# A row of a state-space scan's slot moves from VectorE to GpSimd

## The reference

```python
xn = _layernorm(x)
x_norm = _layernorm(xn, ln_in_g, ln_in_b)
x_norm = x_norm + conv(x_norm)
gate, input_gate = split(x_norm @ gate_w.T + gate_b)
Bm = x_norm * sigmoid(input_gate) @ B_w.T + B_b
Cm = x_norm @ C_w.T + C_b
A_bar = expm(dt_A * A)
def step(state, bc):                 # state: (8, 64)
    b_t, c_t = bc
    s = _layernorm(state @ A_bar + b_t, ln_st_g, ln_st_b)
    return (s, c_t * s)
ssm = scan(step, 0, (Bm, Cm))        # 2048 steps
s = (ssm @ D_w.T + D_b) * sigmoid(gate)
out = x + s * silu(xn @ W.T + b + (xn @ V_r) @ C.T)
```

## Time and profile before

| | us |
|---|---|
| median of 2 executions | 2489.38 (2488.64 to 2490.12) |
| profiled execution | 2491.04 |
| its span | 2489.2 |
| TensorE busy (matmul) | 2448.6 (98%) |
| VectorE busy | 2189.7 (88%) |
| ScalarE busy | 1013.5 (41%) |
| GpSimd busy | 1242.5 (50%) |
| DMA, share of 16 engines | 20% |

### The profile page before, as it was taken

One profiled execution on the slowest core, in us unless ns is written; L12 is line 12 of the kernel. 1 busy time (PEld: TensorE's weight loads), 2 busy tenths in 40 slices (PEclk: granted clock), 3 DMA queues, 4 the chain that ended last, 5 costly groups with the idle time before them and its releaser, 6 DMA issues.

```text
span 2489.2 us, 42423 instructions
## 1 busy us (share of the span) xinstructions
PE 2448.6 (98%) x10031; PEld 1307.4 (53%) x10031; DVE 2189.7 (88%) x10934; ACT 1013.5 (41%) x1859; POOL 1242.5 (50%) x2433
## 2 busy tenths in 40 slices
PE   8999999999999999999999999999999999999996
PEld 4555555555555555555555555555555555555544
DVE  6788889988889988889988899888899888899887
ACT  5444333444433444434443434443344444334310
POOL 2444555545555545555545555445555455555443
PEclk9999999999999999999999999999999999999998
DMA  3112211212212122112122112122112122121121
GB/s 113 24 47 56 60 41 41 52 47 60 57 33 52 48 52 60 45 39 58 49 52 60 43 41 55 48 56 60 38 44 52 47 60 53 36 53 48 35 59 36
DMA packets 99678, 125.14 MB, mean 50 GB/s; under 512 B 31975, under 2 KB 48743, under 8 KB 99432
## 3 DMA queue, kind: packets, MB, share of 16 engines
q1 hardware_dynamic: 98560, 121.12, 20.2%
q10 hardware_dynamic: 872, 1.31, 0.2%
HBM read 71.96 MB, written 33.55 MB: 42 GB/s over the span
## 4 chain that ended last, share of the span: by engine, by line
POOL 33%; PE 33%; DVE 24%; issue 9%; ACT 1%; DMA 0%; POOLq 0%; SPq 0%; DVEq 0%; ACTq 0%
POOL dw L429 30%; DVE wq L942 10%; PE bank L1256 7%; DVE dw L969 7%; DVE dw L955 7%; PE bank L1235 6%; PE bank L1245 5%; PE bank L1323 4%; POOL ln L456 3%; PE bank L1324 3%; PE bank L1266 2%; PE bank L1284 1%; PE bank L1275 1%; PE bank L1186 1%; PE bank L1193 1%
## 5 line engine op out<-in xcount | busy, mean ns | idle before, releaser
L429 POOL TENSOR_TENSOR dw<-q,minus_half 8x1 f32<-8x1 f32 x2048 | 1088.0, 531 | 1187.0 <-DVE wq L942 1153.8
L1323 PEld LDWEIGHTS bank<-Mscan,wT 128*65 128x65 f32 x2046 | 225.7, 136 | 623.9 <-issue 614.5
L1245 PE MATMUL bank<-xnorm,gateT 128*128 128x512 f32 x1024 | 506.2, 593 | 0.9 <-DVE sgT L895 0.9
L942 DVE SCALAR_TENSOR_TENSOR wq<-dw 8x65 f32<-8x65 f32 x2048 | 443.6, 217 | 70.2
L1256 PE MATMUL bank<-xnorm,gateT 128*128 128x512 f32 x1024 | 500.7, 595 | 0.1
L1235 PE MATMUL bank<-xnT,WT 128*128 128x512 f32 x1024 | 494.5, 593 | 0.0
L1323 PE MATMUL bank<-Mscan,wT 128*65 128x128 f32 x2046 | 404.0, 279 | 16.0 <-DVE wT L972 12.6
L1324 PE MATMUL bank<-Mscan,wT 128*65 128x128 f32 x2046 | 391.5, 273 | 0.0
L969 DVE SCALAR_TENSOR_TENSOR dw<-dw 8x64 f32<-8x64 f32 x1024 | 280.2, 274 | 113.1 <-POOL dw L429 87.8
L959 DVE SCALAR_TENSOR_TENSOR dw<-bank,dw 8x128 f32<-8x128 f32 x1024 | 342.9, 335 | 6.7 <-PE bank L1324 5.3
L955 DVE SCALAR_TENSOR_TENSOR dw<-dw 8x64 f32<-8x64 f32 x1024 | 279.9, 273 | 77.1 <-POOL dw L429 75.5
(11 more groups left out here) (188 smaller groups left out, 2742.8 us busy)
## 6 DMA issues: line engine op xcount, KB each, us to landing
xc<-in_x SPq DMA_DIRECT2D x252, 128.0 KB, 2.8
xa<-in_x SPq DMA_DIRECT2D x252, 128.0 KB, 2.7
out<-o SPq DMA_DIRECT2D x248, 128.0 KB, 2.4
dw<-dtok SPq DMA_DIRECT2D x127, 96.0 KB
wtok<-dw SPq DMA_DIRECT2D x128, 33.0 KB
gateT<-in_gateT SPq DMA_DIRECT2D x1, 2048.0 KB
WT<-in_WT SPq DMA_DIRECT2D x1, 1024.0 KB, 7.6
xa<-in_x SPq DMA_DIRECT2D x4, 256.0 KB
```

Of the source, the lines that this page charges most:

```text
L429: nc.gpsimd.tensor_tensor(dw[0:B, t, CR:CR + 1], q[:], minus_half[0:B, 0:1], ALU.pow).then_inc(s["r_ready"], 1)
L942: V.scalar_tensor_tensor(out=wq[:], in0=w_eps, scalar=1.0 / S, in1=w_eps, op0=ALU.mult, op1=ALU.mult, accum_out=q[:]).then_inc(s["q_ready" ...
L1245: ins = mm(mbank["gate", m][:], gateT[:, k, P * m:P * m + P], xnorm[p][:, k, :], start=(k == 0), stop=(k == KH - 1))
L1323: mm(scanP[0:WIDE, 0:2 * S], wT[:, 0:WIDE], Mscan[:, 0, :], start=True, stop=False)
```

## The change

The second row of the odd slot (line 977) is no longer made by VectorE. GpSimd makes it in `step`, behind the power of the even step before: a product of the third row of slot t with r(t) into a new tile `m2r` of 8 x 64, and a sum of that with the second row of slot t + 1. GpSimd's wait for a transfer at steps 14, 30, 46 and 62 of a chunk, for line 959 (`rest_ready`), for its own power and for the previous sum stand ahead of the product, and a wait for the product ahead of the sum. VectorE's waits stay.

```diff
+        m2r = sb("m2r", [B, S])
...
-            p_ready r_ready w_ready q_ready wT_ready rest_ready a_ready
+            p_ready r_ready w_ready q_ready wT_ready rest_ready a_ready m2r_ready
...
                 wait_for(pool, "q_ready", CT, i, t + 1)
                 nc.gpsimd.tensor_tensor(dw[0:B, t, CR:CR + 1], q[:], minus_half[0:B, 0:1],
                                         ALU.pow).then_inc(s["r_ready"], 1)
+                if t % 2 == 0:
+                    if t % QT == QT - 2:
+                        wait_for(pool, D_IN[t // QT], 16, i, 16)
+                    wait_for(pool, "rest_ready", PAIRS, i, t // 2 + 1)
+                    wait_for(pool, "r_ready", CT, i, t + 1)
+                    wait_for(pool, "a_ready", PAIRS, i, t // 2)
+                    nc.gpsimd.tensor_scalar(m2r[:], dw[0:B, t, CM2:SLOT], dw[0:B, t, CR:CR + 1], None,
+                                            ALU.mult).then_inc(s["m2r_ready"], 1)
+                    wait_for(pool, "m2r_ready", PAIRS, i, t // 2 + 1)
+                    nc.gpsimd.tensor_tensor(dw[0:B, t + 1, CM:CM2], m2r[:], dw[0:B, t + 1, CM:CM2],
+                                            ALU.add).then_inc(s["a_ready"], 1)
...
                     if of < NC:
                         wait_for(dve, D_IN[q], 16, of, 16)
-                V.scalar_tensor_tensor(out=dw[0:B, t, CM:CM2], in0=dw[0:B, before, CM2:SLOT], scalar=r,
-                                       in1=dw[0:B, t, CM:CM2], op0=ALU.mult, op1=ALU.add).then_inc(s["a_ready"], 1)
```

## The result

| | before | after |
|---|---|---|
| median, us | 2489.38 | 2956.07 (2955.33 to 2956.80) |
| profiled execution, us | 2491.04 | 2955.33 |
| its span, us | 2489.2 | 2953.5 |

The ratio is 1.1877 (95% interval 1.1857 to 1.1897): 19% slower. The direction was forecast, with 2774 us and a range of 2610 to 2980. The time is inside the range, but the growth is 464 us of span where the sum had 283. So the question of the study is where the other 181 us are.

What follows compares the result with a forecast made beforehand. The prediction took the loop through GpSimd and VectorE to bound the kernel. It added 210 us for product and sum beyond GpSimd's idle time and 73 us for the layer norm to 2491: 2774 us, range 2610 to 2980.

Steps and rivals of the forecast that it cites:

- What bounds: Loop through GpSimd and VectorE (power, first row, sum of squares): 1.17 us a step, 97% of the span.
- rival 3: TensorE in the layer norm's stretch: idle gaps grow, its clock falls to half, about 3000 us; chance 0.04.
- Line 977 at 0: VectorE, odd step: removing line 977 frees nothing on the loop, booked 0; at most part of 12 us of stalls.
- X: GpSimd, even power's end until the odd one can start: 0.85 us; beyond 0.645 all is added per pair, 210 us.
- gap one: GpSimd, from the even step's power to the product: 0.19 us, taken from dependent instructions with a like pattern.
- product: GpSimd's 8x64 product with a column as scalar: 0.25 us, or 0.31 with the other slope; lower bound 0.20.
- gap two: GpSimd, from product to sum, a single wait: 0.06 to 0.20 us, taken as 0.12.
- restart: GpSimd, behind the sum: an independent instruction starts before the one ahead of it ends, -0.03 us.
- Layer norm: GpSimd, steps 34 to 45 of a chunk: small instructions in even steps lose their cover, 73 us together.
- The fulfilled wait: GpSimd, ahead of the product: waits long fulfilled, including the DMA wait at step 14 of a quarter, cost nothing.
- Exclusion (rival 2): Product and sum each wait for VectorE's whole two-input instruction on SBUF: 3020 us; chance 0.20 for 2880 and above.
- What should have shown: Profile after: product 0.15 to 0.20 us behind the even power, intervals 1.38 and 1.17, VectorE idle 0.2 more before line 955.

Runs made afterwards that it cites:

- the four-column kernels: Kernel after with broadcast product and sum on 4 of 64 columns, without and with the layer norm's GpSimd instructions in odd steps: 2561.2 and 2496.3 us.
- the broadcast: Kernel after with the product as an instruction of two inputs, the column r broadcast over 64 columns: 2767.8 us.
- the second four-column one: Kernel after with broadcast product and sum on 4 of 64 columns and the layer norm's GpSimd instructions in odd steps 35 to 57: 2496.3 us.
- product only: Kernel after without GpSimd's sum and the wait ahead of it, VectorE's line 977 back, the product into a tile nobody reads: 2614.0 us.
- the constant: Kernel after with a constant 0.5 instead of the column r as the product's scalar: 2869.9 us.

## Why the prediction was right, and where its sum was off

*What bounds.* Right. The loop of power, first row and sum of squares carries everything; interval times number gives the span's growth within a microsecond. The page's 98% busy for TensorE said nothing on it. Nor did rival 3 happen: over the whole span the granted clock is 0.993, against 0.996 before. A window of 80 us, after (length, busy us of PE, PEld, DVE, ACT, POOL, granted clock, DMA share, GB/s):

```profile
1200.00:1280.00 80.00, 70.52 (x275) 35.07 (x274) 56.38 (x276) 30.58 (x57) 54.80 (x121) 1.00 0.17 43
```

TensorE is down to 88% busy, and the granted clock is 1.00, the level of 2.4 GHz.

*Line 977 at 0.* Right within what the four-column kernels can tell. The traces show a small cost instead of a gain. In steps 31 and 63 of a chunk, where VectorE has no other piece to do, line 955 starts 0.11 and 0.10 us behind the power in the kernel after, the broadcast and the second four-column one, and 0.035 us in the kernel before and in product only, which keeps line 977. That is 63 times 0.07, some 4 us. VectorE's wait for the transfer then stands with no instruction between it and line 955; whether that is the reason was not tested.

*X*, from the end of the even power to the start of the odd one. The structure was right, one term was wrong. Measured against booked: gap one 0.16 against 0.19, product 0.46 against 0.25, gap two 0.08 against 0.12, sum 0.31 against 0.32, restart -0.03 against -0.03; 0.98 against 0.85, and with the power's 0.54 an interval of 1.52 against 1.38. The excess over 1.175 is 0.345 x 1024 = 353 us, where the sum had 210; 0.01 of the 0.345 is the longer power. The product was mis-sized by 0.21, of which the two gaps gave back 0.07. The step that failed is its pricing from a 4-column scaling and the slope of a long memset: that left out the column as scalar (0.08), took 0.86 ns a column where it is 2.5 (0.10), and left out 0.03 that the product takes more in the loop than alone. That 0.03 goes with line 969: in the four late steps of a chunk, where the product starts shortly before line 969 ends, it takes 0.28 us instead of 0.32 in the broadcast kernel and 0.36 instead of 0.39 with the constant, as alone. The nearest row was of a scaling with constants, and the text did not note the difference. Its upper bound for the product, 0.31, failed too. The range held only because its upper end took all four terms at their dear ends, and the other three came out below theirs; that part is luck.

*Layer norm.* 73 booked, 80 measured.

*Odd steps.* Booked at nothing, they cost (1.202 - 1.182) x 1023 = 20 us: some 4 are the starts of line 955 just named, and the power takes 0.55 to 0.56 there instead of 0.53. In the kernels in which GpSimd runs only instructions of two inputs in the loop it takes 0.54 (64 columns) or 0.53 (4), so the change between kinds of instruction is suspected, but was not isolated.

*The fulfilled wait.* "Only the wait for the power itself and the one between product and sum cost anything" was wrong: the wait for the transfer cost 12 us.

Together 353 + 80 + 20 + 12 = 465 us against 464.

*Exclusion (rival 2).* It did not happen, though its time was the nearer one, by chance. The product was not held until line 969 ended: in the pair shown it starts 0.12 us into it; on average it takes 0.461 instead of 0.435, and line 969 keeps its 0.27. Where product and line 942 start together, in the late steps, line 942 takes up to 0.30 instead of 0.22, which is hidden under X. The Trainium skill's rule (SBUF — State Buffer, Who interferes with whom), by which the second of the two to issue is blocked for the whole of the first, is not what these rows show: the two overlap, and one of them is lengthened, the product by 0.03 us (in 32 of 1024 steps by 0.09) or line 942 by up to 0.08.

*What should have shown.* Product 0.16 behind the power: seen. The intervals alternate, but between 1.52 and 1.20 instead of 1.38 and 1.17, and read 2.05 instead of 1.9 with a power of the layer norm. VectorE's idle time ahead of line 955 (now 967) went from 75.5 to 693.2 us, 0.60 a pair rather than 0.2. Of that 0.45 is delay (464 us over 1024 pairs), and 0.15 is work that VectorE no longer does (2189.7 us busy before, 2031.7 after), which the forecast forgot; it is less than the 0.24 of line 977, which overlaps its neighbours. GpSimd's share in the chain of waits can't be read, because the page's chain breaks off for this kernel.

## What to carry to other kernels

When work is moved to an engine that looks half idle, look at where its idle time lies: here it was 0.645 us between two links of a loop, and whatever went beyond it came back 1024 times. Price an added instruction from a row with the same kind of operands, not only the same engine; a scalar taken from memory, 60 columns and one more fulfilled wait were 0.08, 0.15 and 0.09 us. And look at what else used the same idle time, since it loses its cover as a whole.

## What the runs showed of the hardware

- On GpSimd, 8 partitions, alone behind the last step, three of each: scaling 4 columns by a constant 0.211 us, 64 columns 0.359; by a column 0.287 and 0.435. Two inputs of 64 columns 0.310, one of them broadcast 0.282.
- The same product as an instruction of two inputs with the column broadcast is 0.14 us shorter in the loop than as a scaling by a column.
- A fourth wait ahead of GpSimd's product, though long fulfilled, delays its start by 0.1 us. Where the product does not wait for the power (behind the odd power), the same wait delays nothing.
- The 8x1 power takes 0.53 us among its like and 0.55 to 0.56 behind a scaling, or behind a sum that follows one.
- A GpSimd scaling and a VectorE instruction with two inputs from SBUF overlap; neither grew by more than 0.09 us.
